# Key and value projections moved from the state-space network into the recurrence's rounds of a decoder kernel

## The reference

```python
# layer 0, mixer: selective state-space recurrence, 1024 channels, N = 16 states
dt = softplus(dt_raw + b_dt);  dA = exp(-exp(A_log) * dt);  dBu = dt * u * B
h_t = dA_t * h_{t-1} + dBu_t          # over t, for each channel and each n < 16
y   = sum_n C_n * h_n + D * u;  out = (y * silu(z)) @ W_out.T
# layer 0, cross part: autocorrelation of x with ctx (by Fourier matrices), top 9 lags
# layer 0, ffn: dequantised weight plus a low-rank term
# layer 1, mixer: a network of 4 layers, 64 wide: norm, silu, complex decay filter,
#                 norm, 64 -> 256 -> 64
# layer 1, cross attention: 32 query heads, 8 key/value heads of 128
K, V = ctx @ Wkv                      # 1024 x 512 by 512 x 2048, needs ctx only
# layer 1, ffn: one of 8 low-rank experts for each token
```

## Time and profile before

| | us |
|---|---|
| runs | 1477.93, 1477.72, 1473.37 |
| profiled execution | 1475.01, span 1473.2 |
| stage from the first transposes of the recurrence to its end | 127.9 to 551 |
| autocorrelation and ffn, up to the network | 552.2 to 748.8 |
| network, four layers | 748.8 to 900.8 |
| attention and last ffn | to 1473.2 |

### The profile page before, as it was taken

How to read it: one execution, slowest core, us unless ns; L and a number is a source line. 1 busy time by engine, 2 the same in 40 slices (tenths; PEclk the granted TensorE clock), 3 DMA queues, 4 the chain that set the end, 5 groups by cost and what they waited for, 6 DMA issues and landing times.

```text
span 1473.2 us, 18405 instructions
## 1 busy us (share of the span) xinstructions
PE 1317.3 (89%) x6448; PEld 943.2 (64%) x6448; DVE 920.4 (62%) x1671; ACT 746.7 (51%) x1463; POOL 666.4 (45%) x488
## 2 busy tenths in 40 slices
PE   6997877777778889888999998899999899999996
PEld 5885556555566664444465554578888788778774
DVE  5826878778879975788554442554444455555566
ACT  4446998988988870222132222354444344344441
POOL 3229978888888850212641111353333344233321
PEclk9997989999999999999999998799999999999998
DMA  4121000012000023200200000122112122112110
GB/s 146 44 115 58 1 2 0 25 62 86 1 1 1 1 79 88 79 8 1 93 15 29 1 15 22 56 96 72 65 65 73 57 74 78 65 58 72 49 52 29
DMA packets 29546, 71.20 MB, mean 48 GB/s; under 512 B 3376, under 2 KB 3632, under 8 KB 27536
## 3 DMA queue, kind: packets, MB, share of 16 engines
q1 hardware_dynamic: 29456, 70.04, 13.8%
HBM read 67.86 MB, written 2.16 MB: 48 GB/s over the span
## 4 chain that ended last, share of the span: by engine, by line
PE 66%; DVE 13%; ACT 9%; POOL 7%; issue 5%; DMA 1%; SPq 0%; DVEq 0%; POOLq 0%; ACTq 0%
PE psum L457 10%; PE psum L459 9%; PE psum L458 9%; ACT arena L892 6%; DVE arena L1550 4%; POOL arena L1301 4%; PE psum L840 4%; PE psum L524 4%; PE psum L710 4%; PE psum L867 4%; PE psum L704 3%; PE psum L538 2%; ACT psum L892 2%; PE psum L621 2%; PE psum L859 2%
## 5 line engine op out<-in xcount | busy, mean ns | idle before, releaser
L1550 DVE TENSOR_TENSOR_SCAN arena<-psum,arena 128x512 f32<-128x512 f32 x256 | 297.7, 1207 | 82.9 <-ACT psum L892 77.2
L1301 POOL TENSOR_TENSOR arena<-arena 128x1024 f32<-128x1024 f32 x128 | 299.6, 2361 | 65.0 <-DVE arena L1550 65.0
L1233 POOL TENSOR_TENSOR w_split<-arena,w_split 128x512 fp32r<-128x512 f32 x128 | 168.1, 1332 | 310.4 <-ACT w_split L892 310.3
L524 PE MATMUL psum<-prm,arena 128*128 128x128 f32 x1024 | 170.9, 296 | 91.8 <-ACT arena L892 53.5
L524 PEld LDWEIGHTS psum<-prm,arena 128*128 128x128 f32 x1024 | 119.1, 148 | 164.3 <-DVE arena L1550 104.9
L892 ACT ACTIVATE arena<-psum 128x512 f32<-128x512 f32 (+2 forms) x178 | 100.6, 576 | 232.4 <-PE psum L710 53.7
L892 ACT ACTIVATE arena<-psum,ssmn 128x256 f32<-128x256 f32 x480 | 191.4, 500 | 49.2 <-PE psum L524 48.9
L892 ACT ACTIVATE arena<-arena 128x512 f32<-128x512 f32 x96 | 59.3, 629 | 227.2 <-DVE arena L1761 223.6
L892 ACT ACTIVATE psum<-arena,amat 128x508 f32<-128x508 f32 x256 | 171.6, 730 | 1.9 <-DVE arena L1550 1.8
L892 ACT ACTIVATE arena<-psum,prm 128x512 f32<-128x512 f32 (+1 forms) x146 | 98.2, 699 | 116.2 <-PE psum L704 54.3
L538 PE MATMUL psum<-prm,arena 128*128 128x128 f32 x1024 | 142.2, 284 | 0.1
(11 more groups left out here) (221 smaller groups left out, 2434.5 us busy)
## 6 DMA issues: line engine op xcount, KB each, us to landing
arena<-wq SPq DMA_DIRECT2D x64, 256.0 KB, 2.5
arena<-wo SPq DMA_DIRECT2D x64, 256.0 KB, 2.9
arena<-bc_scratch SPq DMA_DIRECT2D x8, 1024.0 KB, 4.6
arena<-win SPq DMA_DIRECT2D x16, 256.0 KB, 2.7
arena<-xT SPq DMA_DIRECT2D x8, 256.0 KB, 6.4
x_tok<-xtok SPq DMA_DIRECT2D x1, 2048.0 KB, 7.8
arena<-wout SPq DMA_DIRECT2D x8, 256.0 KB, 5.5
arena<-ctxtok SPq DMA_DIRECT2D x1, 2048.0 KB, 7.9
```

What stands on the lines that cost most here:

```text
L524: last = nc.tensor.transpose(hT[:, c, b % 2, e, :], hst[:, (2 * k + e) % 4, b * L:(b + 1) * L], ident)
L1233: gp.tensor_tensor(out_, whole, hi.bitcast(F32), ALU.subtract).then_inc(done, 1)
L1301: gp.tensor_tensor(bu[:, i % 4, :, :], dtu[:, (2 * j + e) % 4, :].unsqueeze(1).to_broadcast([P, NG, HT]), Brep[:, q * NG:(q + 1) * NG, :], ...
L1550: v.tensor_tensor_scan(hst[:, i % 4, :], dA[:, i % 3, :], bu[:, (k // NG * 2 + e) % 4, k % NG, :], 0.0, ALU.mult, ALU.add).then_inc(S.scan ...
```

## The change

1. `keys_values` leaves the network and becomes part of the recurrence's rounds: chunk `c` belongs to rounds 4c to 4c+3, with one product in the first, one in the second and two in the third. It accumulates in PSUM bank 2. DVE copies it out in round 4c+4, between the two scans, into one buffer `kv_st`, and SP stores it to device memory (`kt_scratch`, `v_scratch`, 256 KB each time). In the network stage four DMAs bring K and V back (8 MB), behind the autocorrelation's last step.
2. For bank 2 the decays get two banks instead of three, so `decay(i)` waits for scan `i-2` instead of `i-3`.
3. ACT's order in a round: `decay(2k+2)`, `weigh(k-1, 0)`, `decay(2k+3)`, `weigh(k-1, 1)`, where it was both decays and then both parts of `weigh(k)`. PE transposes after both scans of a round, half by half.
4. The operands of the chunks take the place of `x_tok`: half of `ctxT` and half of `wv`, 1 MB each, loaded four and two times; `x_tok` itself is loaded in two halves, in round 96 and behind the last chunk, the second ahead of `ctx_sb` and `four_sb` in SP's order. `OUT_AT` is 90.
5. The second half of `xT` comes with one DMA instead of four.

```diff
-        dA = psum[:, 0:3 * HT].rearrange("p (s t) -> p s t", s=3)
+        dA = psum[:, 0:2 * HT].rearrange("p (s t) -> p s t", s=2)
+        ctxh = x_tok[:, HB:B, :]
+        wvh = x_tok[:, 0:HB, :]
+        wk_sb = row[:, 256:256 + 2 * 512].rearrange("p (s n) -> p s n", s=2)
+        kv_st = row[:, 1280:1280 + 512]
...
+            for c in range(4 * NKV):
+                h, b, half, g_ = kv_chunk(c)
+                sp.wait_ge(S.kv_sb, c + 1)
+                sp.dma_start(kt_dram[h, g_] if b is None else v_dram[b, half], kv_st).then_inc(S.kv_out, 16)
+                if c % (2 * NKV) == HB - 1:
+                    wv_in(1)
...
+                if c == 15:
+                    rows_in(1, 3)
+                    ctx_in(1)
+                    wv_in(0)
+                    wk_in(0)
+                    wk_in(1)
+                if c == 23:
+                    load(x_tok[:, 0:HB, :], xtok[:, 0:HB, :], S.xtok_in0)
+            load(x_tok[:, HB:B, :], xtok[:, HB:B, :], S.xtok_in1)
             sp.wait_ge(S.bu_done, 2 * MD * GS)
             load(ctx_sb, ctxtok, S.ctxtok_in)
...
+            def turn_state(k, c):
+                pe.wait_ge(S.scan_done, 2 * k + 2)
+                if k:
+                    pe.wait_ge(*weighed(k - 1, c))
...
+            def keys_values(c, ks):
+                h, b, half, g_ = kv_chunk(c)
+                if ks[0] == 0:
...
+                    pe.wait_ge(S.ctxh_in, 16 * (h + 1))
...
+                if k % 4 < 3:
+                    keys_values(k // 4, ((0,), (1,), (2, 3))[k % 4])
...
-                if i >= 3:
-                    act.wait_ge(S.scan_done, i - 2)
+                if i >= 2:
+                    act.wait_ge(S.scan_done, i - 1)
...
             for k in range(NR):
                 if k + 1 < NR:
                     decay(2 * k + 2)
+                if k:
+                    weigh(k - 1, 0)
+                if k + 1 < NR:
                     decay(2 * k + 3)
-                weigh(k)
+                if k:
+                    weigh(k - 1, 1)
...
                 scan(2 * k)
-                if k and by_dve(k - 1, 1):
-                    weigh(k - 1)
+                if k and k % 4 == 0:
+                    kv_out(k // 4 - 1)
```

More of the change, by code:

```diff
@@ L36 @@
 NR = 2 * MP * NS
-OUT_AT = 86
+OUT_AT = 90
 ROUTED_FROM = 40
@@ L371, in _ @@
             load(wring[:, 1, :], win[WORD[1]], S.w_in1)
-            for k in range(KD):
-                load(xTh[:, 1, k, :], xT[1, :, k, :], (S.xT_in4, S.xT_in5, S.xT_in6, S.xT_in7)[k])
+            load(xTh[:, 1, :, :], xT[1], S.xT_in4)
             for p in range(2, 16):
@@ L397, in _ @@
-            sp.wait_ge(S.skip_used, MD)
-            sp.wait_ge(S.dtu_done, MD)
-            for m in range(MD):
-                load(wout_sb[:, m, :], wout[m], S.wout_in)
+                if h:
+                    sp.wait_ge(S.bu_done, 2 * ((MP - 1) * GS + 2 * q + 2))
+                load(Brep[:, q * 4:(q + 1) * 4, :].rearrange("p n t -> p (n t)"),
+                     scratch[h, q * 4:(q + 1) * 4, :].rearrange("n t -> (n t)").partition_broadcast(P),
+                     (S.b_in0, S.b_in1, S.b_in2, S.b_in3)[q])
@@ new lines, in ctx_in, with wv_in, wk_in @@
+            def ctx_in(h):
+                load(ctxh, ctxT[:, :, h * HT:(h + 1) * HT], S.ctxh_in)
+            def wv_in(c):
+                load(wvh, wv[:, :, c * 512:(c + 1) * 512], S.wv_in)
+            def wk_in(g_):
+                load(wk_sb[:, g_ % 2, :], wk[g_], (S.wk_in0, S.wk_in1)[g_ % 2])
+            rows_out(0)
+            sp.wait_ge(S.u_done, 2 * MD)
+            for q in range(4):
+                rows_in(0, q)
+            sp.wait_ge(S.inproj, len(UNITS))
+            ctx_in(0)
@@ new lines, in _ @@
+            wv_in(0)
[7 more added lines that the diff above has]
+                    wv_in(1)
+                if c == 5:
+                    rows_out(1)
+                if g_ is not None and g_ + 2 < NKV:
+                    wk_in(g_ + 2)
+                if c == 12:
+                    rows_in(1, 0)
+                if c == 13:
+                    rows_in(1, 1)
+                    sp.wait_ge(S.skip_used, MD)
+                    sp.wait_ge(S.dtu_done, MD)
+                    for m in range(MD):
+                        load(wout_sb[:, m, :], wout[m], S.wout_in)
+                if c == 14:
+                    rows_in(1, 2)
+                if c == 15:
+                    rows_in(1, 3)
+                    ctx_in(1)
+                    wv_in(0)
+                    wk_in(0)
+                    wk_in(1)
+                if c == 23:
+                    load(x_tok[:, 0:HB, :], xtok[:, 0:HB, :], S.xtok_in0)
@@ L411, in _ @@
             sp.wait_ge(S.wout_done, B)
-            load(ctxT_sb, ctxT, S.ctxT_in)
             for k in range(KD):
@@ L421, in _ @@
             load(dw1_sb, dw1, S.dwt_in)
-            load(wv_sb, wv, S.wv_in)
-            for i in range(NKV):
-                if i >= 2:
-                    sp.wait_ge(S.kv_ps, 2 * (i - 1))
-                load(wk_sb[:, i % 2, :], wk[i], (S.wk_in0, S.wk_in1)[i % 2])
+            sp.wait_ge(S.kv_out, 16 * 4 * NKV)
+            sp.wait_ge(S.xat_done, B)
+            for h in range(2):
+                load(KT[:, :, h * HT:(h + 1) * HT], kt_dram[h].rearrange("g p n -> p g n"), S.kt_in)
+            for half in range(2):
+                load(V[:, :, half * 512:(half + 1) * 512], v_dram[:, half].rearrange("b p n -> p b n"), S.v_in)
             sp.wait_ge(S.d_conv, 2 * DEPTH)
@@ L1136, in _ @@
                         last.then_inc(S.d_f, 1)
-                    for h in range(2):
-                        keys_values(1 + KVL * l + 6 + h)
             NU = 2 * NKV
@@ L1555, in finish_y, with kv_out @@
                 v.tensor_tensor(g[:, M, :], bank[6 + M % 2][:, :], g[:, M, :], ALU.mult).then_inc(S.y_done, 1)
+            def kv_out(c):
+                h, b, half, g_ = kv_chunk(c)
+                dve.wait_ge(S.kv_ps, c + 1)
+                if c:
+                    dve.wait_ge(S.kv_out, 16 * c)
+                if b is None:
+                    v.tensor_scalar(kv_st, bank[2][:, :], pc("bk")[:, g_:g_ + 1], None, ALU.add).then_inc(S.kv_sb, 1)
+                else:
+                    v.tensor_copy(kv_st, bank[2][:, :]).then_inc(S.kv_sb, 1)
             ssm_stats(0)
@@ L1572, in _ @@
                 scan(2 * k + 1)
+                if k and by_dve(k - 1, 1):
+                    weigh(k - 1)
                 if w < 3:
```

158 lines of the change are left out of this document (57 added, 101 removed).

## The result

The changed kernel takes 1515.24 us (median of four runs, 1514.58 to 1519.56) beside 1477.83 for the kernel before on the same chip: a ratio of 1.0265, 95% interval 1.0236 to 1.0294. It is slower, where I had forecast 1466 us and a range up to 1494. The profiled execution took 1515.38 us, 40.4 more than the one of before.

The account below looks back on a forecast made before the run. PE was taken to bound the network; in the recurrence four engines stood close, ACT ahead at first. Network -41, first rounds +1, last rounds +19, recurrence's end +10 gave -11 us: 1466 us, range 1453 to 1480, other cases 1436 to 1494.

Parts of the forecast that it names:

- Part 1, the network: Network stage without the key and value products: 41 us saved, between 19 and 52; the largest term.
- I take a layer in which the first half of the products is slow, 28.6 us: Network layer: half clock for the first half of its products only, 9.4 us saved in each of four layers.
- my lower end: Network: half clock all through, a layer 33.5 to 34 us, only 19 us saved.
- the third rival: Network stays at half clock and saves only 19 us: +11 in sum, 1489 us; chance 0.09.
- Part 2, the order: First 86 recurrence rounds: ACT's new order against two decay banks, 12 us saved, between 33 saved and 31 lost.
- I take 12 saved, near the plain rounds: First 86 recurrence rounds: 12 us saved before DMA waits, near the plain rounds, which ran without a pause.
- The second rival: Recurrence: ring of decays and scans binds, 18 lost instead of 12 saved, 5 more in last rounds; 1502 us; chance 0.20.
- the ring: Recurrence: with two decay banks, DVE work between scans holds back the next decay; +24 in sum, 1502 us; chance 0.20.
- The worst case of this part: First 86 recurrence rounds: every DVE copy and all twelve softplus pairs go over to ACT, 31 us lost.
- Part 2, the products: First 86 recurrence rounds: moved products bring PE to 245 us, below ACT's 264 busy us.
- Parts 3 and 4: Last recurrence rounds: 19 us lost, PE has no room; recurrence's end: 10 us lost, waiting for four before spectra.
- the half clock: Network stays at half clock, 19 us saved instead of 41: +11 in sum, 1489 us; chance 0.09.

Follow-up runs that it names:

- e7: Changed kernel with filling 128x512 products that nobody reads put into TensorE's queue where it waits in the network: 1492.63 us, ratio 1.0111.
- e2: Kernel before with the new order alone, three decay banks, keys and values still in the network: 1460.86 us, ratio 0.9886.
- e3: Kernel before with the new order and two decay banks, keys and values still in the network: 1483.20 us, ratio 1.0037.
- e6: Changed kernel with DVE's copy of a chunk behind the second scan of its round instead of between the scans: 1517.30 us, ratio 1.0261.
- e8: Changed kernel with the loads of ctx_sb and four_sb issued behind the store of chunk 30: 1507.40 us, ratio 1.0203.
- e5: Changed kernel with one of the four products of each key or value chunk; copies, stores and loads stay: 1488.72 us, ratio 1.0078.

## Why the prediction was wrong

**Part 1, the network: the largest term, wrong in size; the mechanism was in the text.** The step that failed is "I take a layer in which the first half of the products is slow, 28.6 us". The rows spoke of half clock behind a pause, and I granted the engine its recovery within each layer. It had none: 0.51 over the four layers, 33.1 us each, which was my lower end (19 saved) and the third rival, to which I gave 9 in 100. With the 2.3 us behind the network it gave 21.7 us, not 41. e7 shows that the clock makes the difference: with nothing added to the network but fillers a layer takes 27.3 us.

**Part 2, the order: a gain turned into a loss.** "I take 12 saved, near the plain rounds." The order itself was worth about that in these 86 rounds (10.6 us, e2; 17 in the whole kernel), and the two banks took all of it and more (e3: 303.5 us for 86 rounds against 296.8, so 7 lost): 19 us off. The second rival said this with one of its places (the softplus rounds; of the copies e6 shows 0.7 us in some blocks and nothing in the sum). It said when it decides: over 3.6 us a round before the output projection. That was 339.4 / 90 = 3.77, but not by the ring alone, for e3 has 303.5 / 86 = 3.53. Its 31 us for the first part are what was measured (42.6 less 11.2 for four rounds more), and that is luck: they are 13 of DMA waits and 18 for ring and copies, where ring and order cost 7, and nothing else for the products. Its 1502 us were still too low, since it took the network's 41 us as given. (The worst case of this part, 31 lost, is 30 by its own terms, 21 x 0.67 and 12 x 1.3.) What I had weighed wrongly is the bank: I read in the plain rounds that ACT and DVE run without a pause, where a third bank is of no use, and it is of use only in the others.

**Part 2, the products: costed at nothing.** I compared sums of busy time (PE 245 us, below ACT's 264) and let ACT's work hide PE's. A loop in which PE, ACT and DVE hand each other one round's state isn't bound by a sum: a plain block of four rounds pays 1.4 us for 3.44 of PE work and one copy, although PE then has 10.4 us of work from start to start (4 x 1.75 + 3.44) and ACT 11.2 in a block of 12.5. (Without the products ACT is busy in all of the block's 11.1 us.) Against e3 the 88 rounds cost 22 us, of which I had 13 as DMA waits. The DMA waits themselves were as said to 0.4 us (2.2, 7.3, 2.2). What they cost is another matter: 7 us in round 64, while the blocks with the logarithms (rounds 16 and 80) are no longer than e3's, presumably since ACT is away there anyway.

**Parts 3 and 4: right.** The last 38 rounds took 136.3 us, 134.3 said; in e3 the order gave nothing here either (128.0 us for 42 rounds, 126.8 before), and the products cost their whole time. The wait on `four` was 9.1 + 0.9 us, 7 + 2.6 said; e8 gives 8 to 9 of it back.

The sum of the misses, 19 for the network, 19 for the ring, 9 for the products, makes 47 of the 51 us between -11 and +40; the rest are the 2 us of part 3 and the four rounds before the output projection, which I had at 2.8 us each. The two rivals that came true, the ring and the half clock, stood beside each other in my list as if only one could: both together, by my own numbers, are 1502 + 22 = 1524. What stays open is how far the products cost by their place in PE's order, and how far by the copy and the clock around them, and with that the share of the last quarter of the products against the copies and the traffic in e5's 16 us.

## What to carry to other kernels

Work that fills an engine's pauses may be what holds its clock: before moving it away, price what is left at the lower clock all through, not half of it. In a loop that passes one state from engine to engine, a product laid into it is paid in part long before the engine that does it is full (here 0.2 to 0.4 us of 0.86, the copies included) and in full where that engine has no room; so lay in as few as fit, where a buffer is free, and don't pay for them with a buffer of the loop's own ring. A spare buffer that looks idle in the plain rounds is to be judged in the irregular ones, and together with the order it serves: here it was worth 3 us or nothing in one order and 22 in the other.

## What was not expected of the hardware

The network's PE records filled 88 of 133 us and the granted clock was 0.51, over four layers with waits of up to 4.7 us; with fillers they filled 91 of 109 us at 0.98. The busy share in the records says little, since at half clock the same work fills twice the time. A wait of 2.51 us for a scan, alone, was once followed by the full clock (e2 at 236.57, sums in 1.04 us) and once by the half (e2 at 339.77, sums in 1.77 us): one kernel's trace holds both, and executions of the same code before the recurrence differed by 3 to 4 us with 3 or 16 us at half clock.
